# Two blocks of a mixture-of-experts routing moved into the attention stage before it, and indirect DMAs issued four per group of tiles

## The reference

```python
x = x + tanh(g_xattn[0]) * L0_xattn(layernorm(x), ctx, ctx, ...)      # causal, 16 heads
x = x + tanh(g_ffn[0])   * L0_ffn(layernorm(x), ...)                  # 8 experts, 2 per row
x = x + tanh(g_xattn[1]) * L1_xattn(layernorm(x), ctx, ctx, ...)      # rotary, window of 128
x = x + tanh(g_ffn[1])   * L1_ffn(layernorm(x), ...)                  # 16 experts, 4 per row
```

```python
scores = sigmoid(x @ router.T)                   # 16 experts in 4 groups
# the best 2 groups by the sum of their 2 best scores, then the best 4 experts in them
tw = scores of the 4 chosen; tw = tw / sum(tw) * 2.5
routed = sum over the 4 chosen of tw * down(silu(gate(x)) * up(x))
shared = mlp(x)                                  # for every row, hidden width 256
```

## Time and profile before

| | us |
|---|---|
| median of 3 runs (2158.18 to 2165.54) | 2159.94 |
| the profiled execution | 2160.08 |
| its span, first to last instruction | 2158.3 |
| PE busy | 1654.1 (77%) |
| DVE busy | 1186.3 (55%) |
| ACT busy | 920.0 (43%) |
| POOL busy | 749.6 (35%) |

### The profile page before, as it was taken

The page is one execution under the profiler, slowest core; times in us unless marked ns, Lnnn a source line. Parts: engine busy times, 40 slices in busy tenths (PEclk is TensorE's granted clock), DMA queues, the critical chain, the costliest instruction groups (busy, mean ns, idle before and its releaser), DMA issues. The chain is left out here.

```text
span 2158.3 us, 42333 instructions
## 1 busy us (share of the span) xinstructions
PE 1654.1 (77%) x16024; PEld 1224.5 (57%) x16024; DVE 1186.3 (55%) x2641; ACT 920.0 (43%) x1607; POOL 749.6 (35%) x926
## 2 busy tenths in 40 slices
PE   4799998549999999999469999984548366377573
PEld 3466664338888888888336666653327254255441
DVE  4788888325555555555387887752334245135334
ACT  4478686414444444444135556542205232133220
POOL 2256578671000000000364433311650533422424
PEclk8799999759999999999789999995568788588886
DMA  9753232143545455522153443214334667378763
GB/s 275 185 112 68 59 73 54 37 140 102 175 166 171 152 154 174 174 82 62 59 115 80 82 87 61 58 29 151 100 98 106 173 142 166 95 177 198 179 170 100
DMA packets 394204, 261.08 MB, mean 121 GB/s; under 512 B 319135, under 2 KB 366667, under 8 KB 392728
## 3 DMA queue, kind: packets, MB, share of 16 engines
q1 hardware_dynamic: 367768, 173.06, 32.6%
q0 software_dynamic: 26240, 85.32, 12.3%
HBM read 77.81 MB, written 107.74 MB: 86 GB/s over the span
## 5 line engine op out<-in xcount | busy, mean ns | idle before, releaser
L1379 PE MATMUL ps<-m_xT,m_w_halves 128*128 128x256 f16 x3360 | 419.4, 275 | 13.6 <-issue 11.5
L1379 PEld LDWEIGHTS ps<-m_xT,m_w_halves 128*128 128x128 f16 x3360 | 331.0, 99 | 56.0 <-issue 15.9
L948 ACT ACTIVATE a_probs<-ps 128x1024 f32<-128x1024 f32 (+1 forms) x256 | 234.6, 916 | 180.1 <-PE ps L793 175.8
L1396 PE MATMUL ps<-m_w_halves,m_hiddenT 128*128 128x256 f16 x1680 | 231.8, 274 | 20.0 <-issue 11.5
L1057 POOL TENSOR_TENSOR a_probs<-a_probs,a_half_above 128x512 f32<-128x512 f32 x128 | 162.1, 1269 | 156.0 <-ACT a_probs L948 155.3
L1814 PE MATMUL ps<-m_w_halves,m_rowsT 128*128 x1152 | 164.2, 292 | 61.6 <-issue 51.8
L1694 POOL DMA_INDIRECT m_gathered<-routed_out,m_routed_row x128 | 124.1, 969 | 241.8 <-DMA routed_out<-m_y 128.9
L1357 POOL DMA_DIRECT2D expert_out<-m_y x40 | 28.7, 719 | 511.4 <-DVE m_y L1466 511.4
L1448 ACT ACTIVATE m_hiddenT<-m_hidden 128x256 f16<-128x256 f32 x280 | 116.6, 416 | 186.0 <-DVE m_hidden L1487 185.5
L1490 DVE TENSOR_TENSOR m_hiddenT<-m_hidden,m_hiddenT 128x256 f16<-128x256 f32 x280 | 119.1, 425 | 135.0 <-ACT m_hiddenT L1448 133.6
L1396 PEld LDWEIGHTS ps<-m_w_halves,m_hiddenT 128*128 128x128 f16 x1680 | 162.8, 98 | 47.8 <-DVE m_hiddenT L1490 14.6
(11 more groups left out here) (272 smaller groups left out, 2930.9 us busy)
## 6 DMA issues: line engine op xcount, KB each, us to landing
routed<-m_zeros POOLq DMA_DIRECT2D x32, 768.0 KB, 4.2
routed_out<-m_y SPq DMA_DIRECT2D x48, 512.0 KB
r_w_load<-in_L_w SPq DMA_DIRECT2D x24, 896.0 KB
dispatched<-r_xT SPq DMA_DIRECT2D x10, 1024.0 KB, 7.0
expert_out<-m_y POOLq DMA_DIRECT2D x40, 256.0 KB, 2.6
a_ctx_in<-in_ctx SPq DMA_DIRECT2D x32, 256.0 KB
m_experts_load<-in_L_experts SPq DMA_DIRECT2D x18, 384.0 KB, 3.5
experts_f<-m_experts_halves SPq DMA_DIRECT2D x18, 384.0 KB, 2.8
```

The lines of the kernel that those rows point to most:

```text
L948: A(pr[:, g % 2, 2 * jp:2 * jp + 2, :], SC[:, :, 0:SPAN], ACT.Exp, scale=1.0 / math.sqrt(DH)).then_inc(asem["ex"], 1)
L1379: last = mm(psum[:, v % HB, m * CH:(m + 1) * CH], wh[:, u, ws_, m, d_ * F0 + f_ * P:d_ * F0 + (f_ + 1) * P], xT[:, q % XB, xs_ * KT + d_, ...
L1396: last = mm(psum[:, 4 + 2 * (q % 2) + t, 0:D], hT[:, hs_, f_, t * P:(t + 1) * P], wh[:, u, ws_, 2, f_ * D:(f_ + 1) * D], start=f_ == 0 and ...
```

## The change

1. The routing of the last expert layer's blocks 0 and 1 moves from `moe1` into `attention(1)`, in the slots that `attention(0)` uses for its own routing. The tiles of the routing become `r1[...]`, allocated before `attention(1)`; the DVE chain is cut into five parts of choosing (`route1_choose`) and five of placing (`route1_place`), one part a slot. The score of these two blocks is an exponential on ACT with an addition and a reciprocal on DVE, in place of the sigmoid. The five small tables are loaded, and the DVE tables made, at the head of `attention(1)`.
2. The 64 scatters of these two blocks stand in sequences 11 to 18 of `attention(1)`, one in each slot.
3. The ring of gathered rows in `attention(1)` has 4 sequences in place of 8. The first layer's attention weights are freed before the second attention.
4. The prologue of `moe1` has only the routing of block 2, between the shared jobs. SP issues the loads of the first three shared jobs ahead of the routed weights.
5. In the rounds POOL waits for each round's predecessor to finish its hidden products and then issues at most four indirect DMAs: the scatters of block 2 from round 0, of block 3 from round 10, the gathers of block 0 from round 18, of block 1 from round 28, of block 2 from round 40. The gathers of block 3 follow without pauses. `PAIR_AT` follows; the last four combinations stand behind the last shared job.

```diff
-NB = 8
+NB = 4
+ROUTE_SCATTER1 = {11: (0, 0), 12: (0, 8), 13: (0, 16), 14: (0, 24), 15: (1, 0), 16: (1, 8), 17: (1, 16), 18: (1, 24)}
+ROUTED_SEQS = (14, 8)
...
 # attention, GpSimd
-                    if i % 2 and 0 <= i - 5 < 14 and s in (4, 7):
-                        route_lower(pool, i - 5 + s // 7)
-                    if s % 2 and i in ROUTE_SCATTER:
+                    if i % 2 and 0 <= i - 5 < ROUTED_SEQS[L] and s in (4, 7):
+                        route_lower(pool, L, i - 5 + s // 7)
+                    if not L and s % 2 and i in ROUTE_SCATTER:
                         n, j = ROUTE_SCATTER[i]
                         route_scatter(pool, n, j + s // 2)
+                    if L and i in ROUTE_SCATTER1:
+                        n, j = ROUTE_SCATTER1[i]
+                        if j + s == 0:
+                            pool.wait_ge(rows_ready, n + 1)
+                            pool.wait_ge(x_lo, B + 4 * (n + 1))
+                        route1_scatter(pool, n, j + s, r1["halves"][:, n])
...
 # attention, VectorE
+                    if L and 0 <= n < 2 and 4 <= 8 * (i % 4) + s < 9:
+                        route1_choose(dve, n, 8 * (i % 4) + s - 4)
+                    if L and 0 <= n < 2 and 20 <= 8 * (i % 4) + s < 25:
+                        route1_place(dve, n, 8 * (i % 4) + s - 20)
...
 # attention, ScalarE
+                    if i % 4 == 0 and 0 <= n < 2 and s == 3 and L:
+                        act.wait_ge(lg_done, RG + n + 1)
+                        A(r1["scores"][:, n % 2, :, :], psum[:, 4, 0:RT * E1].rearrange("p (t e) -> p t e", e=E1), ACT.Exp,
+                          scale=-1.0).then_inc(sg_ready, 1)
...
 # moe1
-        PIECES_AT = {2: 0, 3: 9}
-        PAIR_AT = {20: 0, 21: 1, 23: 2, 25: 3, 33: 4, 34: 5, 36: 6, 38: 7, 43: 8, 44: 9, 46: 10, 47: 11}
+        PIECES_AT = {3: 0}
+        PER_GROUP = 4
+        PACED = (("scatter", 2, 0), ("scatter", 3, 10), ("gather", 0, 18), ("gather", 1, 28), ("gather", 2, 40))
+        PAIR_AT = {21: 0, 23: 1, 25: 2, 27: 3, 31: 4, 33: 5, 35: 6, 37: 7, 43: 8, 45: 9, 47: 10, 48: 11}
...
+                for l in range(XB):
+                    load(l)
+                for c in range(4):
+                    sp.dma_start(wh[:, :, c * 4:(c + 1) * 4, :], w16[:, :, c * 4:(c + 1) * 4, :]).then_inc(w_in[1], 16)
...
-                scatter(0)
-                scatter(1)
-                scatter(2)
-                pool.wait_ge(x_lo, 2 * RG)
-                pool.wait_ge(lg_done, RG)
-                gather(0)
-                scatter(3)
-                gather(1)
-                gather(2)
-                gather(3)
+                OPS = RT * K1
+                for r in range(NR):
+                    pool.wait_ge(h_done, H0 + U0 + r)
+                    for what, b, begin in PACED:
+                        first, end = (r - begin) * PER_GROUP, (r - begin + 1) * PER_GROUP
+                        if 0 <= first < OPS:
+                            what_of = scatter if what == "scatter" else gather
+                            what_of(b, first, min(end, OPS))
+                gather(3, 0, OPS)
...
 # moe1, TensorE: the prologue
-                for k in range(4):
-                    round_of_xT(0, k, k)
-                router_logits(0)
                 shared_hidden(0, 0)
                 shared_hidden(0, 1)
-                positions(0)
                 for k in range(4):
-                    round_of_xT(1, k, 4)
-                router_logits(1)
+                    round_of_xT(2, k)
+                router_logits(2)
                 shared_down(0)
...
 # moe1, VectorE: the end
                     lowers_of_job(j)
-                    combine(7 + j)
                 add_job(7)
-                combine(15)
+                for pair in range(12, 16):
+                    combine(pair)
```

More of the change, by code:

```diff
@@ new lines, in flamingo_kernel, with link1, route1_tables @@
+    steps1 = [0]
+    def link1(dve, ins):
+        steps1[0] += 1
+        ins.then_inc(r1_chain, 1)
+        dve.wait_ge(r1_chain, steps1[0])
+    def route1_tables(dve):
+        V, iota = nc.vector, r1["iota"]
+        dve.wait_ge(ld1, 80)
+        V.tensor_tensor(r1["up_to"][:, :, :], iota[:, :].unsqueeze(1).broadcast_to([P, E1, E1]),
+                        iota[:, :].unsqueeze(2).broadcast_to([P, E1, E1]), ALU.is_le)
+        V.tensor_scalar(r1["filled"][:, :], iota[:, 0:RT], float(P), None, ALU.mult)
+        for t in range(QT):
+            V.memset(r1["digit"][:, t:t + 1], float(E1 ** t))
+        for c in range(TILES1 // E1):
+            last = V.tensor_scalar(r1["tile_no"][:, c * E1:(c + 1) * E1], iota[:, :], float(c * E1), None, ALU.add)
+        link1(dve, last)
@@ new lines, in route1_logits, with route1_positions @@
+    def route1_logits(pe, xT, bank):
+        for t in range(RT):
+            for c in range(KT):
+                last = nc.tensor.matmul(psum[:, bank, t * E1:(t + 1) * E1], xT[:, c, t * P:(t + 1) * P],
+                                        r1["router"][:, c, :], start=c == 0, stop=c == KT - 1)
+        return last
+    def route1_positions(pe, n, bank):
+        pe.wait_ge(m1_ready, n + 1)
+        mm, tri, msk = nc.tensor.matmul, r1["tri"], r1["chosen16"]
+        pos = psum[:, bank, 128:256]
+        mm(pos, tri[:, 0, :], msk[:, :, :].rearrange("p t e -> p (t e)"), start=True, stop=False)
+        for s in range(1, RT):
+            mm(pos[:, s * E1:], tri[:, 1, :], msk[:, 0:RT - s, :].rearrange("p t e -> p (t e)"),
+               start=False, stop=s == RT - 1)
+        for t in range(RT):
+            last = mm(psum[:, bank, 256:256 + E1], tri[:, 1, :], msk[:, t, :], start=t == 0, stop=t == RT - 1)
+        return last
@@ L621, in attention, with _ @@
             with nc.Block() as block:
+                @block.sync
+                def _(sp):
+                    for k, name in (("L1_router", "router"), ("L1_e_bias", "e_bias"), ("iota", "iota"), ("less", "less"),
+                                    ("tri", "tri")):
+                        whole = r1[name][:, :] if name in ("e_bias", "iota") else r1[name][:, :, :]
+                        sp.dma_start(whole, a[k]).then_inc(ld1, 16)
                 @block.gpsimd
@@ L1686, in gather, with scatter @@
-                def gather(b):
-                    for u in range(YB):
-                        pool.wait_ge(y_sent[u], 16 * (b + 1) * GROUPS // YB)
-                    for t in range(RT):
+                def scatter(b, first, end):
+                    if first == 0:
+                        pool.wait_ge(rows_ready, b + 1)
+                        pool.wait_ge(x_lo, 2 * (b - 1))
+                    for j in range(first, end):
+                        route1_scatter(pool, b, j, halves(b))
+                def gather(b, first, end):
+                    if b == 0 and first == 0:
+                        pool.wait_ge(x_lo, 4)
+                        pool.wait_ge(lg_done, 2)
+                    if first == 0:
+                        for u in range(YB):
+                            pool.wait_ge(y_sent[u], 16 * (b + 1) * GROUPS // YB)
+                    for j in range(first, end):
+                        t, k = j // K1, j % K1
@@ L1739, in router_logits @@
                     bank4_free()
                     in_bank4.append((sg_ready, n + 1))
-                    for t in range(RT):
-                        for c in range(KT):
-                            last = mm(psum[:, 4, t * E1:(t + 1) * E1], xT[:, c, t * P:(t + 1) * P], router[:, c, :],
-                                      start=c == 0, stop=c == KT - 1)
-                    last.then_inc(lg_done, 1)
+                    route1_logits(pe, xT, 4).then_inc(lg_done, 1)
                 def positions(n):
-                    pe.wait_ge(m_ready, n + 1)
@@ L1855, in _ @@
                 shared_hidden(1, 1)
[L1856 to L1860 removed]
+                shared_down(1)
+                shared_hidden(2, 0)
+                shared_hidden(2, 1)
+                positions(2)
+                shared_down(2)
+                shared_hidden(3, 0)
+                shared_hidden(3, 1)
                 shared_down(3)
@@ L2216, in _ @@
                 lowers_of_job(2)
-                tile_experts(1)
-                weigh(1)
+                for part in range(2):
+                    route1_place(dve, 2, part)
                 add_job(2)
@@ L2221, in _ @@
                 lowers_of_job(3)
+                for part in range(2, 5):
+                    route1_place(dve, 2, part)
                 add_job(3)
```

610 lines of the change are left out of this document (285 added, 325 removed).

## The result

The changed kernel took 2059.76 us (2051.86 to 2065.28, 4 runs) beside 2160.11 (2158.18 to 2165.54, 4 runs): ratio 0.951, 95% interval 0.948 to 0.954. Predicted were 2040, range 1975 to 2125. Its profiled span is 2058.0 us at a mean granted clock of 0.90. One execution of e5 (3022.8 us, clock 0.81) is left out of its median.

The account below looks back on a forecast made before the run. It took GpSimd's long rows of indirect DMAs, delaying TensorE's code, to cost 139 of the rounds' 448 us; 1482.5 + 40 (attention) + 65 (prologue) + 366 (rounds) + 85 (tail) + 1.8 gave 2040 us, range 1975 to 2125.

Parts of the forecast that it names:

- The reason given there: Routed rounds: instructions arrive late while the indirect DMAs' queue is full; seven rows cost 139 of 448 us.
- 10 us of cover: Beside each row of indirect DMAs, code already on the chip covers about 10 us, so a row loses its length less 10.
- Part 1: Last layer's prologue: routing and scatters of blocks 0 and 1 leave it, 65 us against 147.5, saving 82; bounds 55 and 80.
- Part 2: Second attention: the moved routing and scatters cost 40 us there, bounds 13 and 67.
- routing term: Second attention: 13 us for TensorE's transposes, logits and positions, plus 12 for VectorE's routing chain.
- term for rows: Second attention: GpSimd runs ahead and issues three rows of 11 to 16 scatters, each losing 5 us, 15 together.
- Part 3: Routed rounds: four indirect DMAs a round, 40 rounds at 7.9 us and 8 at 6.3, 366 against 448, saving 82.
- Rival 2: Routed rounds: late code costs 0.64 us per DMA whatever the grouping; rounds 405 us, time 2079; chance 0.19.
- Rival 3: Routed rounds: the pause is too short to refill, a paced round takes 11 to 13 us, change slower; chance 0.09.
- Rival 4: Routed rounds: pacing does nothing, something else following the same transfers slows TensorE; rounds 448, time 2122; chance 0.09.
- Part 4: Tail: last four combinations stand behind the last shared job; 85 us against 80.2, costing 5; bounds 74 and 95.
- the sign: Tail: a gap of 20 us or more between the last shared job and the last combinations would show Part 4.

Follow-up runs that it names:

- e5: Changed kernel with block 1's scatters in the rounds, block 0's held by their slot, stores issued by ScalarE; on another chip 1949.4 us, ratio 0.997.
- e1: Changed kernel with a block's indirect DMAs issued in one row of 32 instead of four a round: 2156.5 us, ratio 1.001.
- e11: Kernel before, with its 128 scatters moving 128 bytes a row in place of 1 KB: 2158.9 us, ratio 0.999.
- e2: Changed kernel without scatters in the second attention: block 0's 32 at the last layer's head, block 1's four a round: 2040.5 us, ratio 0.948.
- e10: Changed kernel with block 1's scatters in rounds, block 0's held, finer routing, stores on ScalarE, output transfers behind the last load: 2001.9 us, ratio 0.928.
- e8: Changed kernel with block 1's scatters in rounds, block 0's held, two combinations moved between the last shared jobs; on another chip 1958.1 us, ratio 1.004.

## Why the prediction was right, and where it was not

The total came within 20 us because errors of both signs met: attention +51, prologue +7, rounds -41, tail +4 against the forecast.

**What bounds the kernel before.** Right, for the chips it was read on. e1 gives the loss back with one number, e11 shows that it follows the number of DMAs, not their bytes, and e2's row of 32 cost the 31 us that the row's length less 10 gives.

**The reason given there**, code that arrives late, does not fit the traces. Before, no packet of either instruction queue (q8, q14) is recorded from 1821.0 to 1885.5, that is from 13 us into the row of 48 to 17 us behind its last DMA. The DMA queues from 1821 to 1885, and TensorE's timeline behind the row:

```profile
q0 software_dynamic: 1910, 5.20, 23.4%
q1 hardware_dynamic: 3840, 1.71, 9.7%
```

```profile
1879.68 2.77 PE L1814 MATMUL ps<-m_w_halves,m_rowsT 128*128 x12
1882.24 0.91 PE L1827 MATMUL ps<-ident,m_hidden_halves 128*128 128x128 f16 x8
1882.98 1.47 PE L1814 MATMUL ps<-m_w_halves,m_rowsT 128*128 x12
1884.29 1.47 PE L1788 MATMUL ps<-m_w_halves,m_hiddenT 128*128 x12
```

In that time TensorE crept at 2.8 us a matmul until 1875.4. From 1877.15 it ran 56 matmuls without a pause, and no code had come in between, so by this record they were on the chip while it crept. The same holds in e11 (no packet from 1824.5 to 1887.0) and beside e1's second row (one at 1768, the next at 1795; TensorE free from 1785.27). VectorE's late copy in e1 (1759.85) and ScalarE's late exponential in after (1465.64) did not follow a packet either (none from 1742 to 1768, and none from 1446 to 1468). So it seems that the row holds up instructions that are already there, unless packets are missing from the records. Whether it is their issue or the signals between engines is open: the delays appear on TensorE as "issue", on ScalarE and VectorE as "remote" or "issue", and in e10 on three engines at once. The "10 us of cover" are then a fitted number, not a stock of code: they fit rows of 16 to 48 before the change, and not the attention.

**Part 1** said 65 us, it was 72.3: TensorE's first product started 9.3 us after the attention's end as forecast (1580.92), but its 5 us for eviction chains were too few: TensorE's four waits for VectorE's hidden tiles, ahead of the down products, are 2.22, 4.31, 2.33 and 2.80 us, 11.7 together. The lower clock had been priced. Inside the bounds. TensorE in after, the longest of the four:

```profile
1618.30 4.46 PE L1944 MATMUL ps<-m_w_halves,m_hiddenT 128*128 128x256 f16 x24 [4.31 <-DVE m_hiddenT L2183]
```

**Part 2** is the step that failed: 40 us, bounds 13 and 67, against 91, and the other parts made up for it by luck. Its routing term was 25, measured 33: the products ran slower than half of the earlier trace rows, and the free time of VectorE hid less than was credited. Its term for rows was 15, measured 36. The rows came as forecast (11, 13 and 13 scatters), but the first two alone, within the sequences, cost more than three were to. It carried the 10 us of cover from the rounds over to the attention, but there ScalarE had stopped before the row was 4 us long (1465.64 less 13.21, against 1449.35). And 21 us had no term at all: scatters in GpSimd's queue ahead of the last Newton steps. The prediction named the Newton steps as what paces the scatters, and not the reverse.

**Part 3** had it right that four DMAs and a pause avoid the loss, and a size wrong: 7.9 us a paced round, measured 6.8, so the part saved 118 us and not 82. The 7.2 to 8.7 came from loads beside long rows, which were themselves held up by them; beside a paced row four loads took 5.4 to 5.6 in the rows shown, 5.7 in the median. Rival 2, a price per DMA, is out as stated (it wanted 405 for the rounds), though e10 shows that a paced DMA isn't free. Rival 3 is out: 2 us of pause were enough. Rival 4 is out: the rounds did not stay at 448. The prediction had tied it to the rule of the Trainium skill ("Runtime: NRT & Kernel Launch", section "Instruction fetch mechanics") that fetching is mostly hidden. The traces don't speak against that rule, since no fetch is recorded while TensorE crept; what doesn't follow from it is that spreading the DMAs gains nothing. On the chip of e5 to e8 rows of 32 cost little, and their grouping had little to give.

**Part 4** said 85, it was 88.7. The 10 us for late code were 13.5 (TensorE, 2004.4 to 2017.85, beside the first 16 gathers), so the last addition ended at 54 us, not 50. Behind it VectorE waited 8.55 and 6.49 us for the last gathers, with a combination in between, where the sign named one gap of 20.

## What to carry to other kernels

Where one engine issues indirect DMAs, read the other engines' idle time beside each row, and put a wait every few DMAs before moving any work: here, on one kind of chip, one number was worth 97 us, and one wait per slot some 20 more. What is moved to a queue that nothing paces runs ahead, forms a row, and stands in front of whatever the queue holds last, so its last place has to be priced too. And a gain that comes from a delay of this kind has to be measured on more than one chip.

## What the hardware showed that was not expected

- The same program took 2154 to 2160 us on each chip but one, and 1953.6 there. The difference goes with the delay beside indirect DMAs: in the rounds shown, 2.6 us from a finished tile to its copy on the one kind, 0.04 on the other. Why the chips differ is open, and the kernel before was not traced on the faster one. Part of it lies ahead of the second attention (the first new x at 1147 instead of 1170), which wasn't studied.
- A row of indirect DMAs of 128 bytes a row held the other engines up as long as one of 1 KB (2158.9 against 2158.5 us).
- It holds up TensorE, VectorE and ScalarE alike: TensorE by 2.5 us a matmul in e11, VectorE by 17.0 us in e1, ScalarE by 13.2 in after. It does so while no instruction packet is recorded (60 us without one before).
- A run of 32 matmuls with 16 columns left TensorE at its lower clock in the midst of a busy stage (0.50, 1.44 us for six matmuls that take 0.82).
